# Flamingo-style block: the next group's normalised x transposed by way of DRAM and VectorE instead of TensorE

## What is computed

```python
x = x + tanh(g_xattn) * xattn(layernorm(x), ctx)      # 16 heads of 64
x = x + tanh(g_ffn)   * moe(layernorm(x))             # 8 experts, top 2, hidden 1024

def xattn(h, c):
    q, k, v = h @ Wq, c @ Wk, c @ Wv
    return softmax(q k^T / 8) v @ Wo + bo             # per head, within a batch
```

## Time and profile before

| | us |
|---|---|
| median of 3 runs | 948.61 |
| lowest, highest | 948.35, 949.02 |
| the profiled execution, its own time | 951.25 |
| its span, first to last instruction | 949.5 |
| TensorE busy | 930.2 |
| VectorE busy | 651.6 |
| ScalarE busy | 515.6 |
| GpSimd busy | 276.7 |

### The profile page before, as it was taken

One profiled execution on the slowest core, in us unless ns is written; L12 is line 12 of the kernel. 1 busy time (PEld: TensorE's weight loads), 2 busy tenths in 40 slices (PEclk: granted clock), 3 DMA queues, 4 the chain that ended last, 5 costly groups with the idle time before them and its releaser, 6 DMA issues.

```text
span 949.5 us, 19031 instructions
## 1 busy us (share of the span) xinstructions
PE 930.2 (98%) x7224; PEld 813.0 (86%) x7224; DVE 651.6 (69%) x1536; ACT 515.6 (54%) x1608; POOL 276.7 (29%) x300
## 2 busy tenths in 40 slices
PE   8999999999999999999999999999999999999996
PEld 6788889889889888888898877999999999999995
DVE  4884895895885886867847747665757575757552
ACT  5774684784783774755847624343434343535331
POOL 4911133133133233243022250223232323232222
PEclk9999999999999999999999999999999999999998
DMA  9196320120021021012011015525252626252222
GB/s 250 36 295 141 111 68 29 40 73 34 30 79 57 1 79 58 14 58 65 13 35 46 33 70 169 139 45 139 46 142 42 148 43 148 45 146 48 29 23 23
DMA packets 61019, 73.36 MB, mean 77 GB/s; under 512 B 5870, under 2 KB 53781, under 8 KB 60928
## 3 DMA queue, kind: packets, MB, share of 16 engines
q1 hardware_dynamic: 48640, 55.89, 19.7%
q0 software_dynamic: 12288, 16.25, 9.5%
HBM read 43.23 MB, written 29.49 MB: 77 GB/s over the span
## 4 chain that ended last, share of the span: by engine, by line
PE 92%; DVE 2%; ACT 1%; issue 1%; DMA 1%; POOL 1%; another core or an unknown queue 0%; POOLq 0%; DVEq 0%; SPq 0%
PE out_bank L603 6%; PE probT L590 6%; PE down L1411 6%; PE down L1413 6%; PE down L1412 6%; PE score L615 6%; PE up L1395 6%; PE up L1394 6%; PE up L1396 6%; PE query_bank L531 3%; PE query_bank L533 3%; PE query_bank L532 3%; PE key_bank L557 3%; PE rT L1358 1%; PE key_bank L549 1%; PE key_bank L551 1%
## 5 line engine op out<-in xcount | busy, mean ns | idle before, releaser
L1447 ACT ACTIVATE hid<-up,b 128x512 f32<-128x512 f32 x124 | 85.4, 690 | 199.1 <-PE up L1396 126.1
L1330 POOL DMA_INDIRECT out_dram<-eo,index x64 | 99.7, 1559 | 274.9 <-DVE eo L1517 246.2
L1067 DVE TENSOR_REDUCE negmax<-score 128x4 f32<-128x512 f32 x128 | 82.3, 685 | 41.1 <-PE score L615 41.0
L430 POOL DMA_INDIRECT disp<-packed,slots x56 | 58.3, 1041 | 159.8 <-DMA disp<-packed,slots 105.7
L805 ACT ACTIVATE k_sb<-key_bank 128x512 f32<-128x512 f32 x64 | 38.7, 605 | 118.1 <-PE key_bank L557 116.9
L853 ACT ACTIVATE probs_odd<-score,negmax 128x128 f32<-128x128 f32 x256 | 91.3, 383 | 20.8 <-DVE negmax L1067 20.8
L853 ACT ACTIVATE work<-score,negmax 128x128 f32<-128x128 f32 x256 | 91.5, 385 | 16.7 <-DVE negmax L1067 16.1
L1508 DVE TENSOR_TENSOR hid_l<-hid,hid_h 128x512 fp32r<-128x512 f32 x128 | 88.7, 693 | 4.4
L1075 DVE COPY pT<-probT 128x512 f32<-128x512 f32 x128 | 82.3, 685 | 13.7 <-PE probT L590 13.5
L1517 DVE SCALAR_TENSOR_TENSOR eo<-down,gate,shares_b 128x256 f32<-128x256 f32 x64 | 29.6, 481 | 85.5 <-PE down L1413 85.5
L1506 DVE CAST hid_h<-hid 128x512 fp32r<-128x512 f32 x128 | 54.8, 428 | 37.6 <-ACT hid L1447 36.7
(11 more groups left out here) (314 smaller groups left out, 2753.6 us busy)
## 6 DMA issues: line engine op xcount, KB each, us to landing
disp<-fixed SPq DMA_DIRECT2D x1, 8256.0 KB, 34.2
rows<-disp SPq DMA_DIRECT2D x16, 516.0 KB, 5.0
rows<-x_dram SPq DMA_DIRECT2D x16, 512.0 KB, 5.2
w_raw<-fc1T_dram SPq DMA_DIRECT2D x8, 1024.0 KB, 8.0
w_raw<-fc_dram SPq DMA_DIRECT2D x8, 1024.0 KB, 10.7
out_dram<-rows SPq DMA_DIRECT2D x8, 512.0 KB
c_raw<-ctxT_dram SPq DMA_DIRECT2D x8, 256.0 KB, 4.4
c_raw<-ctxT_dram SPq DMA_DIRECT2D x16, 128.0 KB, 4.9
```

What stands on the lines that cost most here:

```text
L430: pool.indirect_dma_start(out=disp[:, :], out_offset=bass.IndirectOffsetOnAxis(ap=slots[:, j, b:b + 1], axis=0), in_=rows_[:, b, :], in_of ...
L1067: V.tensor_reduce(negmax[:, w % 2, hh * GB:(hh + 1) * GB], score[hh][:, :].rearrange("p (i k) -> p i k", i=GB), axis=AX, op=ALU.max, negat ...
L1330: pool.indirect_dma_start(out=out_rows[:, :], out_offset=bass.IndirectOffsetOnAxis(ap=index[half][:, i:i + 1], axis=0), in_=eo[half][:, i, ...
L1447: nc.scalar.activation(hid[m % 2][:, :], up_bank(n, m)[:, :], ACT.Relu, bias=b1[par][:, m:m + 1]).then_inc(s_hid, 1)
```

## The change

`xn`, once normalised, is written to a new DRAM tensor `normal` (512 rows of 1,024 bytes). When it has landed, eight loads bring it back into `blocks`, which is the memory of `xr`: a load for each quarter (32 columns) of each half of the width. The load puts its 32 columns of token t*32+s on partition q*32+s at place t*32, so each piece has 128 bytes. VectorE then turns each 32x32 block of `blocks` into `xn2T`, one instruction of 128x512 for each half, in step j = 7 between the routing work and `scale_probs(u - 1, 1)`. ScalarE and VectorE split `xn2T`, in SBUF, in place of the two PSUM banks. `FA` and `FB` leave TensorE's list, with the waits on them. This holds for groups 1 to 7; group 0 still has its transposes from `front`. The load of the next x into `xn` now waits for the write (`s_normal_out`), that of `xr` for the turns (`s_turned`) as well, and the loads of `blocks` for the residual that reads `xr` (`s_o_done`).

```diff
@@ misc_of
-    if j == NP - 1:
-        return ["FA", "FB"] if g < NG - 1 else []
@@ gated_block, attention
+    normal = nc.dram_tensor("normal", [TOK, D], f32, kind="Internal").ap()
+    blocks = rows[:, 1].rearrange("p b d -> p (b d)").rearrange("p (k t) -> p k t", k=DK)
@@ SP
         def iteration(g, nxt, has_prev):
             if nxt is not None:
-                sp.wait_ge(s_f_ready, 2 * g + 2)
+                if g == 0:
+                    sp.wait_ge(s_f_ready, 2)
+                else:
+                    sp.wait_ge(s_normal_out, 16 * g)
                 load_x(nxt, 0, s_x_in)
...
                     sp.wait_ge(s_o_done, 2 * g - 2)
+                sp.wait_ge(s_turned, DK * g)
                 load_x(g - 1, 1, s_xr_in)
                 store(g - 1, g)
+
+        def regroup(g):
+
+            sp.wait_ge(s_xn_ready, g + 2)
+            sp.dma_start(normal.rearrange("(b p) d -> p b d", p=P), xn).then_inc(s_normal_out, 16)
+            if g > 0:
+                sp.wait_ge(s_o_done, 2 * g)
+            sp.wait_ge(s_normal_out, 16 * (g + 1))
+            for k in range(DK):
+                for q in range(P // SQ):
+                    d = slice(k * P + q * SQ, k * P + (q + 1) * SQ)
+                    sp.dma_start(blocks[q * SQ:(q + 1) * SQ, k, :].rearrange("s (t d) -> s t d", d=SQ),
+                                 normal[:, d].rearrange("(t s) d -> s t d", s=SQ)).then_inc(s_blocks_in, 16)
...
                      blank[:, :].unsqueeze(1).to_broadcast([P, E * CAP // P, W])).then_inc(s_blank_out, 16)
+        regroup(0)
         iteration(1, 2, True)
+        regroup(1)
         sp.wait_ge(s_w_lo, 3)
         sp.wait_ge(s_w_rest, 4)
         load_expert(sp, fc1T, fc2, 0, w1_raw, w2_raw, s_e0_in)
         for g in range(2, NG - 1):
             iteration(g, g + 1, True)
+            regroup(g)
@@ TensorE
-                if hh == 1 and w % NP == NP - 2 and w < STEPS - 2:
-                    pe.wait_ge(*misc_done("FB", w // NP))
...
-            else:
-                if kind == "FA":
-                    pe.wait_ge(s_xn_ready, g + 2)
-                front(bank, 0 if kind == "FA" else 1)
...
-            if kinds[1:] == ["FB"]:
-                pe.wait_ge(s_pt_done1, w + 1)
-                misc("FB", probT[1], u // NP)
@@ ScalarE
-            if "FA" in kinds:
+            if g < NG - 1 and u % NP == NP - 1:
                 for k in range(DK):
-                    act.wait_ge(s_f_ready, 2 * g + 3 + k)
-                    high(xT_h[:, k, :], (query_bank, probT[1])[k][:, :]).then_inc(s_f_hi, 1)
+                    act.wait_ge(s_turned, DK * g + k + 1)
+                    high(xT_h[:, k, :], xn2T[:, k, :]).then_inc(s_f_hi, 1)
@@ VectorE
             if has_prev and j == 7:
                 route_slots(route, g, g)
+            if has_next and j == NP - 1:
+                dve.wait_ge(s_blocks_in, 16 * DK * (P // SQ) * (g + 1))
+                dve.wait_ge(s_q_ready, NP * (g + 1))
+                for k in range(DK):
+                    V.transpose(xn2T[:, k, :], blocks[:, k, :]).then_inc(s_turned, 1)
             if u > 0:
                 scale_probs(u - 1, 1)
...
-                    low(xT_l[:, k, :], (query_bank, probT[1])[k][:, :], xT_h[:, k, :]).then_inc(s_f_split, 1)
+                    low(xT_l[:, k, :], xn2T[:, k, :], xT_h[:, k, :]).then_inc(s_f_split, 1)
```

More of the change, by code:

```diff
@@ L74 @@
 QUAD = 32
+SQ = 32
 def misc_of(u):
     g, j = divmod(u, NP)
-    if j == NP - 1:
-        return ["FA", "FB"] if g < NG - 1 else []
     if g == 0:
@@ L116, in gated_block @@
         with ExitStack() as ctx:
-            attention(nc, ctx, block, sem, x_v, out_v, disp, ctxT, g_x, g_f, wq, wk, wv, wo, bo, gateT, fc1T, fc2, shared)
+            attention(nc, ctx, block, sem, x_v, out_v, disp, normal, ctxT, g_x, g_f, wq, wk, wv, wo, bo, gateT, fc1T, fc2, shared)
         with ExitStack() as ctx:
@@ L130, in load_expert, with attention @@
     sp.dma_start(w2_raw[:, :, :], fc2[bass.ds(e, 1), :, :].rearrange("o (k p) d -> p (o k) d", p=P)).then_inc(done_sem, 16)
-def attention(nc, ctx, block, sem, x_v, out_v, disp, ctxT, g_x, g_f, wq, wk, wv, wo, bo, gateT, fc1T, fc2, shared):
+def attention(nc, ctx, block, sem, x_v, out_v, disp, normal, ctxT, g_x, g_f, wq, wk, wv, wo, bo, gateT, fc1T, fc2, shared):
     f32, f32r, i32, u32 = mybir.dt.float32, mybir.dt.float32r, mybir.dt.int32, mybir.dt.uint32
@@ L204, in attention @@
         s_dve_self, s_pool_self, s_dve_gate, s_pool_gate, s_e0_in, s_c0_hi, s_e0_hi, s_gc_ready, s_gc_done,
-        s_shift, s_shift2, s_before, s_lt_ready, s_lt_done, s_second, s_minus_mean, s_pair_in, s_beat,
+        s_shift, s_shift2, s_before, s_lt_ready, s_lt_done, s_second, s_minus_mean, s_pair_in, s_beat, s_normal_out, s_blocks_in, s_turned,
     ) = (sem("a_" + name) for name in (
@@ L214, in attention @@
         "dve_self", "pool_self", "dve_gate", "pool_gate", "e0_in", "c0_hi", "e0_hi", "gc_ready", "gc_done",
-        "shift", "shift2", "before", "lt_ready", "lt_done", "second", "minus_mean", "pair_in", "beat",
+        "shift", "shift2", "before", "lt_ready", "lt_done", "second", "minus_mean", "pair_in", "beat", "normal_out", "blocks_in", "turned",
     ))
@@ L225, in misc_done @@
             "LT": (s_lt_done, g), "LX": (s_lg_done, g), "PR": (s_pr_done, g), "GC": (s_gc_done, 1),
-            "FA": (s_f_split, 2 * g + 3), "FB": (s_f_split, 2 * g + 4),
         }[kind]
@@ L666, in misc @@
                 mm(bank[:, 0:E], ones[:, :], gate_sb[:, 1, :], start=False, stop=True).then_inc(s_gc_ready, 1)
-            elif kind == "PR":
+            else:
                 ranks(bank, route, g)
-            else:
-                if kind == "FA":
-                    pe.wait_ge(s_xn_ready, g + 2)
-                front(bank, 0 if kind == "FA" else 1)
         keep_warm(nc, key_bank, ident[:, :], ident[:, :], 22)
@@ L716, in step @@
                 misc(kinds[0], query_bank, u // NP)
-            if kinds[1:] == ["FB"]:
-                pe.wait_ge(s_pt_done1, w + 1)
-                misc("FB", probT[1], u // NP)
-            elif kinds[1:]:
+            if kinds[1:]:
                 pe.wait_ge(s_at_split, w)
@@ L731, in step @@
             if w >= 0:
-                if kinds[1:] and kinds[1] != "FB":
+                if kinds[1:]:
                     pe.wait_ge(*misc_done(kinds[1], u // NP))
```

## The result

| | us |
|---|---|
| before, median of 4 runs (lowest, highest) | 948.48 (948.17, 949.02) |
| after, median of 4 runs (lowest, highest) | 975.99 (974.84, 976.76) |
| ratio after / before, 95% interval | 1.0288, 1.0271 to 1.0306 |
| profiled execution after: own time, span | 976.15, 974.4 |

A forecast was written before the change was run, and what follows sets the result against it. TensorE sets the end, but at borders of groups 1 to 5 the chain VectorE, ScalarE, q_sb sets the time. 30.8 + 3.7 + 4.8 + 0.5 + 2.0 = 41.8 us more gave a forecast of 990, range 975 to 1,024.

The forecast's parts named there:

- group 0, without the clock: Write and loads of blocks wait behind the fill of disp; scores of step 8 at 103.2 instead of 72.44, +30.8 us.
- clock after the wait: After TensorE's idle time in group 0, work starts at half speed: between nothing and 6.6 us, taken as 2 us.
- group 1: Blocks land at 135.4 against VectorE's place at 132.90: 2.5 us late, plus 1.2 for the turns, 3.7 us.
- groups 2 to 5: Blocks land in time with 4.6 us of cover; only the two turns cost, 4 x 1.2 = 4.8 us.
- groups 6 and 7: At the border of group 6 the turns move the scores from 474.57 to 475.1, +0.5 us.
- what is behind the fill waits: On SP's queue in group 0, the write lands only after the 8 MB fill of disp, at 83.1 us.
- The rival in which the write gets past the fill: In group 0 the queue isn't in order for the write; scores at 76.8, total 962 us; chance 0.04.
- the price of 40 ns a piece: Each group's eight loads, 256 pieces per DMA engine at 40 ns, take 10.2 + 1.6 = 12 us.
- the write lands before 81: Sign that the prediction is wrong: the normalised x's write in group 0, forecast near 83, lands before 81 us.
- The sum at the low end: Low end of the range: loads 5.7 us, two turns 0.7, no clock loss; +27 us, 976.
- rival (c): A 128-byte piece costs twice one of 1 KB, 134 ns: 36 us per group, total 1,150 us; chance 0.10.
- The rival with TensorE alone: TensorE alone counts and every microsecond freed at the seven borders is gained: 6.6 us less, 942; chance 0.02.

The follow-up runs named there:

- Experiment 3: Changed kernel with four loads of 128 KB per group in place of eight of 64 KB, same 4,096 pieces: 975.66 us, ratio 1.0287.
- experiment 2: Kernel before plus two unused VectorE turns: 955.04 us; changed kernel, disp fill early, transfers kept but TensorE's transposes in place of turns: 948.97 us.
- experiment 4: Changed kernel with 84 unused matmuls put into TensorE's wait in group 0: 975.31 us, ratio 1.0278.
- Experiment 7: Load of the residual's x held longer: on experiment 6 with finer waits 947.47 us, ratio 0.9989; on the kernel before 948.24 us, ratio 0.9993.
- experiment 1: Changed kernel with the fill of disp issued 26 us earlier: 954.75 us, ratio 1.0067; same move on the kernel before: 948.85 us, ratio 0.9999.
- experiment 6: Changed kernel, disp fill early, from group 2 normalisation in j = 2, turns in j = 5: 952.25 us; with finer border waits too: 948.03 us.

## Why the prediction was right, and where its sizes were off

| term | predicted | measured |
|---|---|---|
| group 0, without the clock | 30.8 | 20.1 |
| clock after the wait | 2.0 | 1.2 |
| group 1 | 3.7 | 1.2 |
| groups 2 to 5 | 4.8 | 4.8 |
| groups 6 and 7 | 0.5 | 0.2 |
| sum | 41.8 | 27.5 |

**Group 0.** The step "what is behind the fill waits" is shown: the write is issued at 51.2 and lands 1.3 us behind the fill, and with the early fill group 0 lasts 51.48 us, as long as before (51.58). The rival in which the write gets past the fill is refuted. Two sizes inside the term were off. The blocks came at 84.65 instead of 95.3: 4.3 us because the write landed at 78.76, not 83.1, and 6.3 because the loads, with the 0.2 us ahead of them, took 5.9 us, not 12.2. The first came from taking the fill's own 34.2 us and the x load's 17.5 as fixed, though after the change the fill lands 31.1 us from its issue; why it is quicker was not tried. The second is the largest error: the price of 40 ns a piece. It leaned on the load of `gate_sb`: 16 pieces an engine in at most 0.78 us, 49 ns each or less, though 0.58 of the 0.78 is the distance of the two issues. Experiment 3 gives at most 21 ns. The prediction's own bound from below, 5.7 us, was within 0.2 of the 5.9: it had 4.1 to the last issue and 1.6 for its landing, measured are 3.6 and 2.3. So with eight loads the issues make up most of the time.

By its own signs the prediction was wrong in one point: it said so if the write lands before 81, and it landed at 78.76. That sign was set on the fill's old duration, and what failed is this size, not the order of the queue. A second sign, that border steps get shorter, holds for step j = 7 alone (7.69 to 6.59); the two steps together got longer.

That the time is still inside the range is partly luck. The sum at the low end, 976, took quick loads (5.7), turns of 0.35 us and no clock loss. The loads were so quick, but the turns and the clock cost more than that, and the write, fixed at 83.1 in the whole range, came 4.3 us sooner. These errors cancel.

The Trainium skill ("DMA: Bandwidth & Descriptors", Anatomy of one DMA) gave an estimated 7 us for a group, which the prediction set aside; the trace has 5.9, so its estimate was nearer than the row, though experiment 3 shows that neither the number of issues nor that of pieces sets the time alone. The rule of the Trainium skill on pieces below 512 bytes (same page, Specifications), as rival (c) read it, would have cost 36 us a group; a group took 5.9.

**Group 1.** Its term had 2.5 us for late blocks. The write lands 3.0 us after its issue at 139.44, not 5.3, the loads go out at 142.52 and are there before VectorE's place, 154.2: no wait. Only the turns' 1.2 remain.

**The turns.** The duration of a turn was a choice between 0.35 and 0.71, by the row of the subtraction. It is that: 690 ns in the median of 14, 0.61 us from start to start. The choice was the prediction's own, and it came out: 1.2 us a border is right at groups 1 to 5, and experiment 2 gives the turns alone 1.17. The chain from release to scores, 7.9 us, is 7.87 with the clock at full speed (experiment 4).

**Group 6.** The two steps around the border grew by 0.34 us (14.11 to 14.45) and the step behind them by 0.1, together near the 0.5. The rest is a gain that the prediction did not see: in the profile of after GpSimd is idle during the normalisation of that group, which lasts 1.38 us for 2.76, and the step is 0.24 us shorter. Experiment 7 shows this cause on the kernel before.

**The clock.** The mechanism was right, and the 2.0 us, a value taken between nothing and 6.6, were too high: 1.2, by experiment 4.

**The rival with TensorE alone,** 942 us, is refuted: without any wait on a DMA the kernel still takes 954.75. TensorE's 92% of the chain did not mean that its work in this place was the pace. In the profile after, the two waits named came out at 0.64 us for the second subtraction (1.6 forecast, because the transposes of probabilities wait first, 0.68) and 0.53 for `q_sb` (0.9 forecast).

## What to carry to other kernels

A transfer put on a queue costs what stands ahead of it: look for the largest transfer that can be outstanding at its first use, not at its own duration. Moving the large one earlier helps only as far as it has landed by then. Work moved off the engine that is busy 98% gains nothing where another engine's chain releases it; the price is read from the starts of the same instruction over two steps, where one gets shorter and the next longer. Work moved off a busy engine and on to the chain that sets the pace costs its full duration. A price for a small piece should not be taken from a transfer so small that its fixed time fills it; such a row is an upper bound, here more than twice the value.

## What the runs showed of the hardware

A transfer that loads pieces of 128 bytes is quick here: 64 KB in 512 pieces land in 2.3 us in the median, and 4,096 pieces over 16 DMA engines in 5.9 us with eight issues and 5.3 with four (experiment 3). A plain store of 512 KB lands in 3.0 us in the median of after, less than a load of x of the same size, 5.2 before and 4.1 after.

SP itself, not only the transfer, is held: the issue of the write lasted 19.61 us behind the fill. It ends at 70.8, 6.7 us before the fill lands, so SP comes free before the fill is through. With the early fill the issue lasts 0.37 (experiment 1), though the write then still takes 6.7 us to land.

VectorE's small instructions with two operands in SBUF grow when they meet one of GpSimd's additions: 0.18 to 0.72 us, 0.16 to 0.34 and 0.15 to 0.70 in experiment 6, while the reduction between them stays at 0.25. In that trace the three long ones end at 400.38, 401.05 and 401.74, and additions end at 400.33, 401.03 and 401.72: each ends 0.02 to 0.05 us behind an addition. The Trainium skill ("SBUF — State Buffer", SBUF: two separate sides) says that an instruction of VectorE with two SBUF inputs and one of GpSimd that reads SBUF lock each other out of a shared pair of ports for a whole instruction; these rows agree, the one operand of the reduction included. The normalisation, four instructions with one large operand each, grows too, from 1.38 to 2.76 us; what that sentence says of two inputs does not cover it, and which rule does was not tried.
